# Four transformer layers on one core: first loads in finer pieces, layer 0's norms in two pieces, the last feed-forwards with buffers of their own and a two-piece output, under a new hand-set order

## What is computed

```python
mod = (_silu(L3_c) @ L3_wmod).reshape(L3_c.shape[0], 6, 1, -1)
h = _layernorm(x, axis=-1) * (1 + ca) + sa
x = x + ga * _L3_attn_ref(h, ...)
h = _layernorm(x, axis=-1) * (1 + cb) + sb
x = x + gb * _L3_ffn_ref(h, ...)
```

```python
last = hidden_states[:, -1, :]
logits = gelu(last @ Wp1 + bp1) @ Wp2 + bp2
sel = jnp.argmax(softmax(logits))
h = gelu(hidden_states @ W1[sel] + b1[sel])
reasoned = h @ W2[sel] + b2[sel]
return hidden_states + 0.3 * (reasoned @ Wo + bo)
```

## Time and profile before

| | us |
|---|---|
| runs, median of 3 | 1881.79 |
| lowest and highest | 1880.4 and 1886.44 |
| the profiled execution's own time | 1882.58 |
| its span, first to last instruction | 1880.8 |

### The profile page before, as it was taken

One profiled execution on the slowest core, in us unless ns is written; L12 is line 12 of the kernel. 1 busy time (PEld: TensorE's weight loads), 2 busy tenths in 40 slices (PEclk: granted clock), 3 DMA queues, 4 the chain that ended last, 5 costly groups with the idle time before them and its releaser, 6 DMA issues.

```text
span 1880.8 us, 31901 instructions
## 1 busy us (share of the span) xinstructions
PE 1777.1 (94%) x10330; PEld 1346.4 (72%) x10330; DVE 1241.5 (66%) x4280; ACT 1097.6 (58%) x2685; POOL 1277.5 (68%) x1770
## 2 busy tenths in 40 slices
PE   5999999999999999999989899999999999898997
PEld 3878898766666566666756567777788976786964
DVE  5964435788778868887688745334577745768673
ACT  5343524666886687767766686543455556445455
POOL 5556757899789978988799887102267755655554
PEclk9999999999999999999999999999999999999998
DMA  8000000010000000000000000000000011000001
GB/s 296 1 18 2 2 1 3 2 47 1 1 1 1 1 1 1 1 1 1 1 1 1 1 9 10 1 1 4 2 3 1 3 30 32 2 1 2 1 13 56
DMA packets 23993, 26.18 MB, mean 14 GB/s; under 512 B 3196, under 2 KB 20868, under 8 KB 23444
## 3 DMA queue, kind: packets, MB, share of 16 engines
q1 hardware_dynamic: 23828, 24.15, 4.1%
HBM read 22.00 MB, written 2.15 MB: 13 GB/s over the span
## 4 chain that ended last, share of the span: by engine, by line
PE 61%; POOL 21%; ACT 6%; DVE 6%; issue 5%; DMA 1%; SPq 0%; POOLq 0%; DVEq 0%; ACTq 0%
PE ps L86 55%; POOL arena L103 19%; PE ps L89 5%; ACT arena L97 5%; DVE arena L103 2%; POOL arena L106 1%; DVE arena L106 1%; ACT L97 1%; DVE arena L109 1%; DVE arena L123 0%; DVE arena L141 0%; DMA rows<-in_rows 0%; DVE sgn L106 0%; DVE arena L126 0%; DMA arena<-in_L_ffn_W 0%
## 5 line engine op out<-in xcount | busy, mean ns | idle before, releaser
L103 POOL TENSOR_TENSOR arena<-arena 128x128 f32<-128x128 f32 (+5 forms) x800 | 741.0, 940 | 371.5 <-DVE arena L109 197.6
L97 ACT ACTIVATE arena<-ps 128x128 f32<-128x128 f32 (+10 forms) x1096 | 366.0, 368 | 458.8 <-PE ps L86 323.9
L86 PE MATMUL ps<-arena 128*128 128x128 f32 (+4 forms) x2864 | 463.5, 296 | 21.2 <-DVE arena L103 5.8
L86 PEld LDWEIGHTS ps<-arena 128*128 128x128 f32 x2864 | 381.5, 192 | 113.2 <-issue 49.1
L103 DVE TENSOR_TENSOR arena<-ps,arena 128x128 f32<-128x128 f32 (+4 forms) x688 | 300.9, 449 | 208.8 <-PE ps L86 196.2
L97 ACT ACTIVATE arena<-arena 128x128 f32<-128x128 f32 (+1 forms) x768 | 299.0, 442 | 60.4 <-POOL arena L103 51.8
L97 ACT ACTIVATE arena<-ps,cols 128x512 f32<-128x512 f32 x324 | 218.1, 688 | 155.1 <-PE ps L86 145.1
L86 PE MATMUL ps<-arena,cst 128*128 128x360 f32 (+1 forms) x768 | 291.1, 493 | 15.1 <-POOL arena L103 7.1
L86 PE MATMUL ps<-arena,moe 128*128 128x256 f32 (+1 forms) x960 | 289.4, 442 | 2.0 <-DVE arena L103 1.0
L89 PE MATMUL ps<-cst,arena 128*128 128x128 f32 x1388 | 238.6, 276 | 31.7 <-ACT arena L97 17.9
L89 PEld LDWEIGHTS ps<-cst,arena 128*128 128x128 f32 x1388 | 166.6, 141 | 92.8 <-issue 31.1
(11 more groups left out here) (110 smaller groups left out, 1937.3 us busy)
## 6 DMA issues: line engine op xcount, KB each, us to landing
rows<-in_rows SPq DMA_DIRECT2D x1, 2253.0 KB, 9.9
arena<-in_x SPq DMA_DIRECT2D x4, 512.0 KB, 9.0
wf<-in_wf SPq DMA_DIRECT2D x2, 1024.0 KB, 12.7
arena<-in_L_ffn_W SPq DMA_DIRECT2D x8, 256.0 KB, 2.8
out_dram<-arena SPq DMA_DIRECT2D x4, 512.0 KB, 3.3
wmod<-in_wmod SPq DMA_DIRECT2D x4, 384.0 KB, 9.6
arena<-kept SPq DMA_DIRECT2D x24, 64.0 KB, 3.1
arena<-kept SPq DMA_DIRECT2D x8, 192.0 KB, 3.0
```

The costliest lines, as they stand in the source:

```text
L86: return UNSENT if self.e is None else self.e.matmul(out, lhsT, rhs, start=start, stop=stop)
L97: return self.e.activation(out, in_, func, bias=bias, scale=scale)
L103: return UNSENT if self.e is None else self.e.tensor_tensor(out, a, c, op)
```

## The change

It has five parts and a new table.

1. `queue_first` loads `ct` alone first, then half of element 0's `x`, `wmod`, the identity apart from the other constants, the other half, `rows0`, `w0`, `cols` and the other elements' `x` in halves. `sm`, the masks, `wmod` of layer 1 and the long `rows` come behind the gates. Waits name the finer pieces (`ident`, `ct`, `x{b}_{h}`).
2. In layer 0 `stats` and `scales_pool` run for 4 tiles at a time, so POOL handles 8 groups of 4 and not 4 of 8. ACT norms all four tiles of group 0, the DVE only tile 7.
3. The scratch of the common bias work (`three`, `left`, `fold`) moves from the arenas' ends into `wf1` and `wf2`, whose loads then wait for it on SP's queue.
4. `Ffn2` and `Ffn3` get `xn` of 1024 columns, `Ffn3` also `hid` and `rT` for both groups. Group 1 (later tokens) is normed and transposed first. In layer 3 the transposes back precede both groups' products. POOL adds the bias, the gain and the normed part to `x` ahead of time (`f3start`, three operations), and the DVE ends with two: product times 0.3 times gain, plus `x`.
5. `queue_out` sends each half of an element's `x` when its `f3x` is done.

```diff
 def queue_first():
-    load("sm", sm[:, :], A["wsmall"])
+    load("ct", ct[:, :], A["ct"])
+    load("x0_0", room[0].x[:, 0:4, :], xv[0, :, 0:4, :])
     load("wm0", wmod[:, 0, :], A["wmod0"])
-    load("x0", room[0].x, xv[0])
-    load("cst", cst[:, :], A["cst"])
+    load("ident", ident, A["ident"])
+    load("x0_1", room[0].x[:, 4:8, :], xv[0, :, 4:8, :])
...
 def common_act():
-    act.wait_ge(*arrives("sm"))
-    act.act(sil[:, :], wsm("ct"), ACT.Silu)...
+    act.wait_ge(*arrives("ct"))
+    act.act(sil[:, :], ct[:, :], ACT.Silu)...
+    yield
     act.wait_ge(*arrives("rows0"))
...
 def l0_dve(b):
-    dve.wait_ge(*arrives(f"x{b}"))
-    yield from stats(b, [(r.x[:, t, :], t) for t in range(NT)])
-    yield from scales(b, "l0stats", b)
+    for h in range(2):
+        dve.wait_ge(*arrives(f"x{b}_{h}"))
+        yield from stats(b, [(r.x[:, t, :], t) for t in range(4 * h, 4 * h + 4)])
+        yield from scales(b, "l0stats", b, h)
...
 def l3f_dve(b):
-    dve.tt(four(tmp), four(ps[:, :]), over(row("bo3f")), ALU.add)...
+    dve.stt(tmp, four(ps[:, :]), 0.3, over(r.row(5)), ALU.mult, ALU.mult)...
-    dve.stt(tmp, tmp, 0.3, m.xn, ALU.mult, ALU.add).then_inc(*dve.up(b, "f3y", b, g))
+    dve.tt(xg, xg, tmp, ALU.add).then_inc(*dve.up(b, "f3x", b, g))
 def l3f_pool(b):
-    pool.wait_ge(*at("f3y", b, g))
+    pool.wait_ge(*at("f3xn", b, g))
+    pool.wait_ge(*at("bo3part"))
+    pool.tt(tmp, tmp, over(row("bo3f")), ALU.add).then_inc(*pool.up(b))
...
-    pool.tt(xg, xg, tmp, ALU.add).then_inc(*pool.up(b, "f3x", b, g))
+    pool.tt(xg, xg, tmp, ALU.add).then_inc(*pool.up(b, "f3start", b, g))
 def queue_out(b):
-    for other in ("pe", "dve", "act", "pool"):
-        sp.wait_ge(*at("left", "l3f", b, other))
-    load(f"out{b}", ...)
+    for g in range(2):
+        sp.wait_ge(*at("f3x", b, g))
+        load(f"out{b}_{g}", ...)
 TURNS = {
-    "pe": ("0123440000000002233002202220002113300022112133311222300013330001110022330111000231110003332211100011"
```

362 lines of the change are left out of this document (187 added, 175 removed).

## The result

The changed kernel takes **1872.83 us** (median of 5 runs, 1870.8 to 1873.61), the kernel before 1881.79 (5 runs, 1880.4 to 1886.44). The ratio is 0.9944, with an interval of 0.9929 to 0.9959: 0.56% faster, more than the 0.3% that can be told from no change. The forecast was 1865.5 (1855 to 1878), so the sign was right, the time lies in the range, and the gain was forecast 1.8 times too large (16.3 us for 9.0). The profiled execution after has a span of 1871.1 us instead of 1880.8, 9.7 less where the sum had 16.3.

What follows compares the result with a forecast made beforehand. PE, busy for 94% of the span, was taken as the bound, its 103.7 us idle as what counts. 1882.6 - 5.9 - 1.5 - 3.8 - 3.1 - 2.0 = 1866.3; the runs' median being 0.8 lower, 1865.5 us, range 1855 to 1878.

Steps and rivals of the forecast that it cites:

- The forecast's own case: Whole kernel: the summed gains hold and the time is 1860 to 1872 us; chance 0.58.
- rival A: Layer 0: the DVE has as much work as before, so the start's 5.9 us are given back, 1871.4; chance 0.12.
- Start: Up to the DVE's first attention operation: earlier norms bring it from 33.19 to 27.3 us, 5.9 gained (3 to 8.4).
- Layer 2's feed-forward: Second group no longer waits for its buffer, so PE waits less on ACT at transposes: 1.5 us gained (0 to 2.7).
- The middle: Between the two ends: the new order removes part of PE's idle time, 2 us gained (12 gained to 14 lost).
- rival B: Middle: the new order removes 8 to 12 us of idle time instead of 2, 1855 to 1860; chance 0.14.
- rival C: Layer 1: each of 16 blocks waits some 0.7 us more, 11 us lost, 1878.5; chance 0.11.
- rival D: Layer 1's long stage: POOL sets it, a start 23 us later lengthens the run, 1890.5; chance 0.05.
- The end up to the last matmul: Element 2's expert choice: load waits and slow clock go, transposes move ahead, less new waits: 3.8 us gained (0 to 5.6).
- the 1.7 for the clock: End: the half-speed stretch of nearly 4 us behind the wait for the expert's load goes, 1.7 us gained.
- Behind the last matmul: Closing chain: POOL's 2.6 us go and the last transfer is halved, 3.1 us gained (2.6 to 3.6).
- The 0.5 for the halved transfer: Behind the last matmul: the last output transfer has 256 KB instead of 512, gained besides POOL's 2.6 us.

Runs made afterwards that it cites:

- experiment 1: Changed kernel with transfers issued in the old order; element 0's x still in halves, identity still apart: 1872.92 us, 0.9948.
- experiment 2: Changed kernel with 55 small ACT operations of unused result in front of its first norms: 1871.19 us, 0.9943.
- experiment 7: Changed kernel with matmuls of unused result added in PE's waits of the first 20 us: 1870.46 us, 0.9935.
- experiment 4: Kernel before, with only own buffers for both halves in the feed-forwards of layers 2 and 3, order unchanged: 1883.43 us, 1.0005.
- experiment 5: Changed kernel with layer 3's closing operations as before, POOL multiplying and adding at the end: 1878.52 us, 0.9978.
- experiment 6: Changed kernel with each element's output sent in one piece of 512 KB: 1870.47 us, 0.9936.
- m1: Changed kernel's code, but from 45 to about 1700 us the steps in the order of the kernel before: 1895.26 us, 1.0069.

## Why the prediction was right, and where it was too large

The direction was right because its two ends held, and the time fell into a range that is 23 us wide. The forecast's own case (1860 to 1872) was missed by 0.8 us, and rival A's 1871.4 is nearer to the measured 1872.8 than the forecast's 1865.5; A is refuted by its mechanism alone, not by the time. By its steps, in us of the profiled span:

- **Start, forecast 5.9, measured 4.4 at the first attention operation and 4.2 at 131.7 us.** The chain up to the first norms came as worked out: `wmod` at 5.25 (5.0 taken), norms at 13.29 (13.3), transposes at 14.99 (15). Of the 8.4 us by which the norms come earlier, 5.9 are ACT's and the DVE's order and the halves, 2.5 the order of transfers (experiment 1). The step that failed is the next: from the first norms to the DVE's first operation I had 14.0 us of ACT's queue plus three matmuls, and it took 15.5. The failed assumption is that ACT works "in a row": its work up to the last copy was 12.4 us (13.1 taken), but it stood still for 2.5, 0.4 for POOL ahead of the norms at 15.34 and 2.1 for PE ahead of four copies (at 18.26, 23.19, 26.63 and 27.48). The half speed of PE in these 15 us, which I had not put in, is 0.4 of the miss; it is no difference between the two kernels, since both have it. PE's idle time in the first 50 us is 15.6, near the forecast's 17. That the lead is then kept through layer 0 was right by 131.7 us, and shifts of the start by -1.5, -2.1 and 0.4 us (experiments 1, 2 and 7) are passed on, so rival A fell, though its mechanism is in the trace: PE waits 3.3 us for the DVE between 50 and 100 us.
- **Layer 2's feed-forward, forecast 1.5, measured 0.** Shown by experiment 4, for the order before. I had taken PE's waits on ACT ahead of transposes for waits on a buffer. The lower bound, "if they were ACT's queue", was the case. The forecast's test, PE's waits on ACT at its transposes down to about 1 us, was even met in the changed kernel (0.5), and yet PE idles 5.2 us in 1500 to 1600 us, against 4.2 before: it now waits for ACT at products (1.8) and for the DVE at transposes (1.5). A test on one kind of wait does not show that time was won.
- **The middle, forecast 2.0, measured 0.4 together with the feed-forward.** The forecast's own test was idle time of about 65 us between 50 us and 60 us ahead of the end, and it is 64.3. But it is made of a loss of 4.6 to 688.5 us and a gain of 5.0 behind it (the lead goes from 4.2 to -0.4 to 4.6). Each kernel has two stretches in between (at 812.8 and 1382.8 before, at 793 and 1640 after), and those after cost 1.8 together. Experiment 2, which has none there, goes from 2.2 to 5.3; of the 2.7 it gains more, 1.8 are the stretches and 0.9 is drift. All five runs of the same order gain more here than the changed kernel's trace (its 0.4 plus 1.5, 2.7, 0.7, 1.7 and 2.2 for experiments 1, 2, 5, 6 and 7). So the order's worth in the middle lies between 0.4 and 3.1 us from one execution to the next, the forecast's 2.0 alone lies inside, its 3.5 with the feed-forward does not, and some of this miss is the execution that was profiled. Rivals B, C and D fell. D least of all: POOL in the long stage is busy for 625 us instead of 616, and PE's idle time there is the same.
- **The end up to the last matmul, forecast 3.8, measured 2.7.** The wait for the expert's weights shrank from 3.0 to 0.4 as forecast, and the blocked DVE operation that I had taken back appeared. The 7.6 us of cover were right (six products, one group with `wo3f`, one of transposes, 7.2 us in the trace from 1837.63 on), though the text lists more than it adds up. The failed step is the 1.7 for the clock. I had taken the half speed for time lost and tied it to the wait for the load. Experiment 4 shows that without it the kernel before wins only 0.3 us, since PE then waits 1.10 us for the next weights. And in the changed kernel the load's wait went, but a stretch came 30 us earlier, at 1821, behind a wait of 0.96 us for the DVE, and cost 0.7; in experiments 5 and 6, which lack it, this piece is 4.0 and 3.3. The test "no granted clock of 0.50 in the last 40 us" fails by its letter, since the record has 0.50 from 1868.9 us to the end; but PE has no work there. The stretch that cost time, 1821 to 1824.5, lies 47 us ahead of the end, outside the test.
- **Behind the last matmul, forecast 3.1, measured 2.4.** POOL's 2.6 are gone. The 0.5 for the halved transfer is nothing (experiment 6), and from the last issue to the end it is even 4.4 us instead of 4.1 before, which puts the term 0.2 under its own lower bound of 2.6 (the upper one, by its own figures, is 3.5 and not 3.6). That the output's split does nothing I had refused as a case of its own, and it is what happened to that part.

The misses are 1.7, 3.1, 1.1 and 0.7, together the 6.6 us between the sum's 16.3 and the 9.7. All four have one sign, so no miss covered another: for the feed-forward and the halved transfer I took a value inside where the bound of no gain was the answer.

## What to carry to other kernels

With a fixed order on every engine, time won at the start arrives at the end, and so does time lost: in m1 4.4 us of lag were still 4.2 us 1600 us later. It follows that two orders can't be joined, even where all engines have done the same work, without looking for the small setup steps each order has put somewhere else; m1's second seam cost 13.0 us within 28, more than the whole change gained. A wait on an engine is not a wait on the buffer that this engine fills: before a buffer is doubled, see whether the engine's queue was empty. Time at half clock is not time lost: before it is put into a sum, see what the engine would wait for next. And moving two operations off a last chain is worth their time only if the engine left behind has room for the rest of its pairs.

## What the runs showed of the hardware that was not expected

- TensorE's stretches at 1.2 GHz after the start last 3.4 us (6.8 and 13.7 at m1's seams), follow waits of 0.4 to 2.5 us, and change place from one execution to the next: the changed kernel's at 793 us is at 408 in experiment 1 and nowhere in experiment 2. The same wait of 2.5 us is followed by one in the kernel before and not in experiment 4. One costs 0 to 1.4 us, and drift comes on top, so traces of single executions of one order differ by up to 2.4 us for no reason in the code.
- The clock's record can begin late: in the kernel before at 31.1 us and in experiments 1, 2, 4 and 6 at 25 to 31. Up to there a window shows 1.00 whatever the clock was.
- From the last output's issue to the end of the span it is 4.0 to 4.4 us in all kernels (4.0 to 4.2 with whole elements, 4.3 to 4.4 with halves), while 256 KB land in 2.4 and 512 KB in 3.3. SyncE waits for every transfer's arrival one after the other at the end, and the kernel with halves has more such waits; that this list sets the end was not tried.
- An ACT operation on 128x1 numbers takes 0.20 us alone and 0.095 in a row of 55.
- A small DVE operation (1x8) beside POOL's 128x512 additions takes 1.07 to 1.25 us instead of 0.22, in every one of the three cases of the changed kernel's choice; each ends 0.02 us behind the POOL operation that it overlaps. The Trainium skill (GPSIMD Engine Reference, Key points) says that POOL and the DVE share SBUF interfaces and contend where the DVE's instruction is in a two-port mode or has two SBUF inputs. The trace agrees for two inputs: the DVE's addition of two SBUF tiles at 1853.68 takes 1.29 us beside POOL and 0.69 at 1862.33 behind POOL's last, while two operations with one input in PSUM at 1857.28 take 1.29 together beside POOL. The small operation has one input, and no row shows its mode.
